# One block with the first shared pairs inside attention's last steps, and the second expert's result added by its transfer

## What is computed

```python
h = concat([patch_embed(x), text_embed(x_txt)])         # (64, 229, 128)
h = h + attn(layernorm(h))
t = layernorm(h)
# experts: 2 shared ones see every token, of 8 routed ones each token sees its 2 best
shared = sum_n gelu(t @ sw1[n].T + sb1[n]) @ sw2[n].T + sb2.sum(0)
probs  = softmax(t @ gate_w.T + gate_b);  top_v, top_i = top_k(probs, 2)
routed = sum_e cw[t, e] * (gelu(t @ rw1[e].T + rb1[e]) @ rw2[e].T + rb2[e])
out = h + shared + routed
```

## Time and profile before

| | |
|---|---|
| span of the profiled execution | 1363.1 us |
| that execution's own time | 1364.89 us |
| TensorE busy | 1231.9 us (90%) |
| VectorE | 1009.1 us (74%) |
| POOL | 830.3 us (61%) |
| ScalarE | 827.3 us (61%) |
| attention | 0 to about 581 us |
| early pairs | 590 to 799 us |
| routed tiles | 799 to 1204 us |
| late pairs | 1192 to 1363 us |

### The profile page before, as it was taken

The page is one execution under the profiler, slowest core; times in us unless marked ns, Lnnn a source line. Parts: engine busy times, 40 slices in busy tenths (PEclk is TensorE's granted clock), DMA queues, the critical chain, the costliest instruction groups (busy, mean ns, idle before and its releaser), DMA issues.

```text
span 1363.1 us, 39403 instructions
## 1 busy us (share of the span) xinstructions
PE 1231.9 (90%) x11910; PEld 1010.8 (74%) x11911; DVE 1009.1 (74%) x2599; ACT 827.3 (61%) x1969; POOL 830.3 (61%) x824
## 2 busy tenths in 40 slices
PE   4999999999999998257999989999999999998997
PEld 2777877777777886235777778888888888966676
DVE  3688788778788787238777757777777777789997
ACT  1566566565656665153444447777777777756664
POOL 3345776676767765667777616676676676753331
PEclk7999999999999999668999999999999999999999
DMA  5233334343333312124444222222222322236663
GB/s 153 81 126 112 116 117 128 100 132 114 120 113 125 127 60 69 61 81 132 121 115 119 73 57 81 83 84 81 82 84 76 86 81 80 64 99 179 187 179 106
DMA packets 119520, 142.62 MB, mean 105 GB/s; under 512 B 18591, under 2 KB 98782, under 8 KB 119417
## 3 DMA queue, kind: packets, MB, share of 16 engines
q1 hardware_dynamic: 95800, 101.42, 25.6%
q0 software_dynamic: 19584, 33.45, 8.1%
q10 hardware_dynamic: 4032, 6.57, 1.9%
HBM read 86.38 MB, written 55.96 MB: 104 GB/s over the span
## 4 chain that ended last, share of the span: by engine, by line
PE 45%; DVE 7%; issue 3%; ACT 2%; DMA 0%; POOL 0%; DVEq 0%; ACTq 0%
PE bank L1615 4%; PE bank L1637 4%; PE bank L1636 4%; PE bank L1638 4%; PE bank L1616 4%; PE bank L1617 4%; PE bank L1081 3%; PE bank L1080 3%; PE bank L1079 3%; PE bank L1033 2%; PE bank L1034 2%; DVE hid_all L1062 2%; PE bank L1035 2%; DVE hid_all L1064 2%; PE bank L1603 2%
## 5 line engine op out<-in xcount | busy, mean ns | idle before, releaser
L1334 POOL DMA_INDIRECT y_dram<-y_sb,y_row x244 | 273.1, 1119 | 154.5 <-issue 74.5
L1041 ACT ACTIVATE gel_all<-bank,b 128x458 f32<-128x458 f32 x256 | 157.1, 641 | 161.8 <-PE bank L1035 148.5
L1411 ACT ACTIVATE gel_all<-bank,b 128x256 f32<-128x256 f32 x488 | 192.9, 473 | 54.1 <-PE bank L1617 30.3
L1081 PE MATMUL bank<-w_hi,hid_all 128*117 128x128 f16 (+1 forms) x1024 | 181.5, 221 | 0.0
L1080 PE MATMUL bank<-w_lo,hid_all 128*117 128x128 f16 (+1 forms) x1024 | 181.4, 221 | 0.0
L1079 PE MATMUL bank<-w_hi,hid_all 128*117 128x128 f16 (+1 forms) x1024 | 181.4, 221 | 0.0
L1636 PE MATMUL bank<-w_hi,hid_all 128*128 x976 | 173.1, 220 | 0.0
L1637 PE MATMUL bank<-w_lo,hid_all 128*128 x976 | 170.5, 219 | 0.0
L1638 PE MATMUL bank<-w_hi,hid_all 128*128 x976 | 170.5, 219 | 0.0
L1534 DVE CAST hid_all<-gel_all 128x1024 f16<-128x1024 f32 x122 | 85.4, 700 | 103.3 <-ACT gel_all L1411 103.3
L1323 POOL DMA_INDIRECT slots_dram<-rows_s,slot_2nd x128 | 133.6, 1044 | 39.6 <-issue 38.3
(11 more groups left out here) (185 smaller groups left out, 3266.8 us busy)
## 6 DMA issues: line engine op xcount, KB each, us to landing
xin<-in_xmain SPq DMA_DIRECT2D x32, 771.8 KB
rows_r<-slots_dram SPq DMA_DIRECT2D x122, 130.0 KB
x2r_dram<-rows_1st SPq DMA_DIRECT2D x32, 260.0 KB, 2.6
rows_s<-x2r_dram SPq DMA_DIRECT2D x32, 260.0 KB, 2.7
scratch<-y_dram SPq DMA_DIRECT2D x32, 234.0 KB
x2t_dram<-x2T SPq DMA_DIRECT2D x32, 229.0 KB, 2.9
scratch<-y_dram SPq DMA_DIRECT2D x32, 224.0 KB
x_cols<-x2t_dram ACTq DMA_DIRECT2D x28, 229.0 KB, 2.7
```

The lines of the kernel that those rows point to most:

```text
L1081: last = pe.matmul(dst, lo, self.w_hi[:, w], start=False, stop=f == self.NG - 1)
L1334: pool.indirect_dma_start(out=y_dram, in_=y_sb[:, s, c, :], in_offset=None, out_offset=bass.IndirectOffsetOnAxis(ap=y_row[:, s, c:c + 1], ...
L1411: act.activation(gel[:, s8 % 2, f, :], up_bank[s8 % 2][half][:, (f % 2) * TILE:(f % 2 + 1) * TILE], ACT.Gelu, bias=b1[:, bass.ds((e + SHAR ...
```

## The change

- Both functions no longer open a block; they return each engine's function, and one block calls them one behind the other. The barrier between them goes. What the second part needs of the first, it now waits for by that part's semaphores.
- `steps` takes a function `between`, called behind steps 30 and later. SyncE loads the columns of pairs 0 and 1 behind step 30. Behind step 31 come pair 0's eight ups, gelus and four splits (now all on VectorE), behind step 32 the whole of pair 1 (`tensor_pair`, `vector_pair`), with pair 0's downs. VectorE's last `slots` and TensorE's last `rank` are in step 33, so behind pair 1.
- The two bias rows of the second layer (`b2`) are loaded and summed in attention's first steps, all on POOL (`sum_biases`, behind step -2); VectorE's part of it goes.
- In the second part VectorE's tables are cut into pieces between pairs 2, 3, 4, 5 and 6. POOL, not VectorE, clears `scratch`. `tag_rows` runs two rows later in the pairs, and SyncE writes the tails of the regions behind the load of pair 16, not 6.
- `rows_s` is now the same buffer as attention's `rows_1st`, so `load_rows` of the first four waits for attention's scatters. The PSUM banks are dealt out differently, so that pair 0's ups use banks that attention has left.
- `load_y` loads only the first result of each token; POOL issues a transfer that adds the second one (`accum_op`) in place of the sum.

```diff
-        embed_and_attend(nc, bank, ...)
-        experts_and_combine(nc, bank, ...)
+        attend, done = embed_and_attend(nc, keep, bank, ...)
+        experts = experts_and_combine(nc, keep, done, bank, ...)
...
+        @block.vector
+        def _(dve):
+            attend["vector"](dve, experts["vector_between"])
+            experts["vector"](dve)
...
             for i in range(hi, PAIRS + 4):
                 step(i, i % 2, i // 2, i % 4)
+                if between is not None and i >= PAIRS - 2:
+                    between(eng, i)
...
+            def sum_biases():
+
+                own = Own(pool, b2_up)
+                s0, s1 = EXPERTS * HID, (EXPERTS + 1) * HID
+                own.did(pool.memset(b2[:, :], 0.0))
+                pool.wait_ge(b2_loaded, 64)
+                own.did(pool.tensor_tensor(b2_in[:, s0:s1], b2_in[:, s0:s1], b2_in[:, s1:B2_COLS], ALU.add))
+                own.wait()
+                own.did(pool.tensor_copy(b2[0:B2_LO, :], b2_in[0:B2_LO, 0:s1]))
+                own.wait()
+                own.did(pool.tensor_copy(b2_high[B2_LO:, :], b2_in[B2_LO:, 0:s1]))
+                own.wait()
+                own.did(pool.tensor_tensor(b2[B2_LO:2 * B2_LO, :], b2_in[B2_LO:, 0:s1], b2_high[B2_LO:, :], ALU.subtract))
...
+    def up_free(self, pe, k, f):
+
+        if self.before is not None and isinstance(k, int) and k < 2 and f < (3 if k == 0 else 4):
+            if k == 0:
+                pe.wait_ge(self.before.sil, 5 * PAIRS)
+            else:
+                pe.wait_ge(self.gel_ready, self.NG)
+                pe.wait_ge(self.before.mid_ready, PAIRS)
+        elif self.before is not None and isinstance(k, int) and k == 0:
+            pe.wait_ge(self.gel_ready, f - 2)
...
+        def sync_between(sp, i):
+            if i == PAIRS - 2:
+                for k in range(2):
+                    sp.wait_ge(done.t_out[k], 16)
+                    early.load(sp, k, k)
...
+                else:
+                    sp.wait_ge(done.scattered[b], 64 * PAIRS // ROW_BUFS)
+                    sp.wait_ge(done.r_out[b], 16 * PAIRS // ROW_BUFS)
...
-                    sp.dma_start(y[0:n, b, :, c], y_v[i, at:at + n]).then_inc(y_in[b], 16)
+                    sp.dma_start(y[0:n, b, :, c, 0:HID], y_v[i, at:at + n, :, 0:HID]).then_inc(y_in[b], 16)
...
+            pool.memset(scratch[:, 1024:], 0.0).then_inc(scratch_up, 1)
...
-                both_y = y[:, b].rearrange("p i c w -> p (i c) w")
-                pool.tensor_tensor(both_y[:, :, 0:HID], both_y[:, :, 0:HID], both_y[:, :, HID:], ALU.add).then_inc(summed, 1)
+                for c, (at, n) in enumerate(CHUNKS):
+                    pool.dma_start(y[0:n, b, :, c, 0:HID], y_v[i, at:at + n, :, HID:], accum_op=ALU.add).then_inc(summed[b], 16)
...
+        def scalar_between(act, i):
+            if i == PAIRS - 1:
+                act.wait_ge(done.w_late, 16)
+                for f in range(NG):
+                    early.gelu(act, 0, f)
+                act.wait_ge(done.t_out[0], 32)
+                early.load(act, 2, 0)
...
+        def vector_between(dve, i):
+            if i == PAIRS - 1:
+                for j in range(NJ):
+                    early.split(dve, 0, 0, j)
+            if i == PAIRS:
+                vector_pair(dve, 1, 1)
...
+            dve.wait_ge(done.top_kept, PAIRS)
             dve.tensor_tensor(expd, top8[:, :, :], top8[:, :, 0:1].to_broadcast([P, NCH, 8]),
                               ALU.subtract).then_inc(centred, 1)
...
             dve.tensor_copy(tag_2nd[:, :, 1], expd[:, :, 1]).then_inc(tags_up, 1)
+            pair(2, 0)
...
+        def tensor_between(pe, i):
+            if i == PAIRS - 1:
+                pe.wait_ge(done.ws_done, PAIRS)
+                for f in range(NG):
+                    early.up(pe, 0, 0, f)
+            if i == PAIRS:
+                pe.wait_ge(done.b2_up, B2_STEPS)
+                tensor_pair(pe, 1, 1)
```

More of the change, by code:

```diff
@@ L15 @@
+from collections import namedtuple
 from contextlib import ExitStack
@@ L58 @@
 B2_LO = 32
+B2_COLS = (EXPERTS + SHARED) * HID
+B2_STEPS = 5
 EARLY_PAIRS = 18
@@ new lines, in build, with _ @@
+        block = keep.enter_context(nc.Block())
+        @block.sync
+        def _(sp):
+            attend["sync"](sp, experts["sync_between"])
+            experts["sync"](sp)
+        @block.gpsimd
+        def _(pool):
+            attend["gpsimd"](pool)
+            experts["gpsimd"](pool)
+        @block.vector
+        def _(dve):
+            attend["vector"](dve, experts["vector_between"])
+            experts["vector"](dve)
+        @block.scalar
+        def _(act):
+            attend["scalar"](act, experts["scalar_between"])
+            experts["scalar"](act)
@@ L271, in reaches, with steps @@
             return not isinstance(n, int) or n >= k
-        def steps(eng, step):
+        def steps(eng, step, between=None):
             lo, hi = 8, PAIRS - 8
@@ L327, in step, with gpsimd @@
                     store_x2(i - 1, 1 - p, (q - 1) % 4)
-            steps(sp, step)
-            for parity in range(2):
-                sp.wait_ge(t_out[parity], 16 * PAIRS // 2)
-            for buf in range(ROW_BUFS):
-                sp.wait_ge(r_out[buf], 16 * PAIRS // ROW_BUFS)
-                sp.wait_ge(scattered[buf], 64 * PAIRS // ROW_BUFS)
-            sp.wait_ge(w_late, 16)
-        @block.gpsimd
-        def _(pool):
+            steps(sp, step, between)
+        def gpsimd(pool):
             pool.memset(rel[:, :, :], 0.0).then_inc(zeroed, 1)
+            pool.memset(b2_in[:, 0:B2_COLS], 0.0).then_inc(b2_zeroed, 1)
             pool.memset(ident[:, :], 0.0).then_inc(const_p, 1)
@@ L461, in _, with vector @@
             steps(pool, step)
-        @block.vector
-        def _(dve):
+        def vector(dve, between):
             own = Own(dve, setup_v)
@@ L701, in _, with scalar @@
                                      op0=ALU.mult, op1=ALU.subtract).then_inc(uvw_ready, 1)
-            steps(dve, step)
-        @block.scalar
-        def _(act):
+            steps(dve, step, between)
+        def scalar(act, between):
             act.wait_ge(w_in, 16 * N_W)
@@ L819, in step, with tensor @@
                     weights_hi(i, p)
-            steps(act, step)
-        @block.tensor
-        def _(pe):
+            steps(act, step, between)
+        def tensor(pe, between):
             def text(grp):
@@ L998, in _ @@
             pe.wait_ge(setup_v, 9)
-            steps(pe, step)
+            steps(pe, step, between)
+    done = Done(t_out, r_out, scattered, ws_done, top_kept, slots_up, mid_ready, sil, x2T_ready, routed, lg_read, w_late, b2_up)
+    return {"sync": sync, "gpsimd": gpsimd, "vector": vector, "scalar": scalar, "tensor": tensor}, done
 class SharedExperts:
@@ L1005, with __init__ @@
     NJ = NG // 2
-    def __init__(self, nc, ctx, tag, first, flip, bank, acc, w_hi, w_lo, b1, b2, ones, x_cols, gel, hid, x2t_dram):
+    def __init__(self, nc, keep, tag, first, flip, up_bank, down_bank, acc, w_hi, w_lo, b1, b2, ones, x_cols, gel, hid, x2t_dram,
+                 before=None):
         def sem(name):
-            return ctx.enter_context(nc.semaphore(f"{name}_{tag}"))
+            return keep.enter_context(nc.semaphore(f"{name}_{tag}"))
         self.first, self.flip, self.acc, self.x2t_dram = first, flip, acc, x2t_dram
@@ L1296, in _ @@
             pool.memset(fill[:, :, HID:HID + 1], UNUSED).then_inc(filled, 1)
-            pool.memset(ones[:, :], 1.0).then_inc(set_up, 1)
             pool.iota(tile_no[:, :], pattern=[[1, TILES]], base=0, channel_multiplier=0,
@@ L1454, in _, with vector_pair, vector @@
             scale_y(PAIRS - 1)
-        @block.vector
-        def _(dve):
+        def vector_pair(dve, i, parity):
+            for j in range(NJ):
+                early.split(dve, i, parity, j)
+                if j == 2:
+                    early.accumulate(dve, i - 1, 0)
+            early.accumulate(dve, i - 1, 1)
+        def vector_between(dve, i):
+            if i == PAIRS - 1:
+                for j in range(NJ):
+                    early.split(dve, 0, 0, j)
+            if i == PAIRS:
+                vector_pair(dve, 1, 1)
+        def vector(dve):
             own = Own(dve, own_s)
```

272 lines of the change are left out of this document (120 added, 152 removed).

## The result

The changed kernel takes **1345.43 us** (median; 1344.18 to 1346.26), the kernel before 1364.57 in the same comparison: a ratio of 0.9862, 95% interval 0.9845 to 0.9879. The forecast was 1331, in a range of 1320 to 1352. So the time is in the range, but of the 34 us that the sum promised 19 came.

The account below looks back on a forecast made before the run. TensorE was taken as the bound, busy 90% of the span, with time to win only at the seam and in the last eighth. 22 us there plus 12 late made 34, so 1331 us from 1364.53, range 1320 to 1352.

Parts of the forecast that it names:

- rival (c): Seam: moved slots hold POOL and ScalarE longer, or the clock stays low; 12 us instead of 22, 1341 us; chance 0.13.
- seam wait of 24.2 us: Between the two blocks: TensorE waits for the second block's first columns, behind the barrier; the change was to remove it.
- one wait in pair 2: Seam: TensorE stands some 13 us at up(2, 4), for ScalarE's gelus behind the tags.
- first transpose: Start of the tiles: TensorE's first tile transpose was to come at 776 to 778.
- late period: Last stage: time per late pair was to be 10.6 to 10.8 us.
- they now begin ... 598.3 ... so its last one ends about 5 us before its 776.3, at 771.2: Seam: POOL's second-choice rows begin at 598.3 instead of 603.36, and end about 5 us earlier.
- up(3, 4): Early pairs after the seam: TensorE was to reach this up at 613.2 instead of about 639.4, gaining 26.2 us.
- if tags throttle TensorE ... 15: Seam, lower bound: tags throttling TensorE, or a clock slower to return, leave 15 us.
- 0, and 0 to 2 as bounds: Attention's start: bias loads and sums moved to the front cost 0, with 0 to 2 us as bounds.
- I take off 2: gain 12: Last stage: of at most 14.0 us, 2 go to the adding transfers' latency; gain 12, between 5 and 14.
- rival (a): Last stage: adding transfers become the bound, or five y buffers can't cover their latency; 1343 to 1363 us; chance 0.14.
- rival (b): Last stage: adding transfers cost from 2.55 us each, making the kernel slower; 1394 us at 3 us each; chance 0.06.

Follow-up runs that it names:

- rows_first: Changed kernel with SyncE's first four row loads ahead of the fill and POOL's scratch memset behind the first two pairs' scatters; 1346.35 us, ratio 0.9861.
- tails_last: Changed kernel with the eight fills of the regions' ends behind the last row load, run twice; ratios 0.9889 and 0.9882, second median 1350.78 us.
- ten_y: Changed kernel with ten half-width buffers for the experts' results in the same memory instead of five; 1340.22 us, ratio 0.983.
- y_plain: Changed kernel with POOL's 64 transfers overwriting instead of adding, so half of each expert sum is left out; 1339.95 us, ratio 0.9823.

## Why the prediction was right in sign and range, and its gain too large by 14 us

The time lies in the stated range, but outside what the forecast itself was given (1326 to 1339) and inside what rival (c) was given (1336 to 1346).

**Right: where the bound was, and that it moved.** The seam wait of 24.2 us and the table stall went, in their place came one wait in pair 2. The order at attention's end ran as followed, 3 to 5 us late throughout: the last slots at 586.8 (predicted 583.5), POOL's last first-choice row done at 597.6 (593.7), the first gelu of pair 2 begun at 604.8 (599.8: the prediction's 600.4 is its end), TensorE's wait 15.6 us (13). The four pieces of the tables cost TensorE at most 1.5 us of waiting (from 640 to 660), and the cast and the subtraction fell back to nearly their early times. Of the signs that were named, the first transpose (776 to 778, came at 791.3) and the late period (10.6 to 10.8 us, came at 11.0) were missed.

**Wrong: "they now begin ... 598.3 ... so its last one ends about 5 us before its 776.3, at 771.2".** This is the step that failed. It was right that POOL bounds the tiles' start; both terms of its chain were mis-sized. The start was 603.19, 4.9 late: 3.9 because the slots and the rows ahead of it were late, mostly attention's own 4.3, and 1.0 because the row load landed after about 4 us instead of the 2.7 of the earlier trace rows, and POOL waited for its tag. And the 128 transfers took 180.7 us from first to last, not 172.9: I took over the 1044 ns of the earlier trace rows, measured in the old order of work. In the new order the same transfer took 1109. The landing of the last row took 0.8 more than I allowed. That is 4.9 + 7.8 + 0.8 = 13.5 us, and tile 0 was issued at 787.36 instead of 773.9. What TensorE gained at up(3, 4) could not matter, for the reason that rows_first shows: TensorE is paced by POOL through the tags, and gives back what it gains. ScalarE began gelu(3, 4) at 619.2, 21.0 us earlier than before (26.2 was predicted, and 26.4 used in the next sum by a slip); at the tiles 8.3 were left. I had named this as a bound of the range ("if tags throttle TensorE ... 15"); the seam gave 12.6 by itself and 8.3 with the start, so the size is that of rival (c), 12 us; of its two reasons the late slots had a share, and the slower transfers were not among them.

What goes with the longer transfers can be read from the rows. In the changed kernel their mean is 1252 ns from 603 to 623 us and 1173 from 643 to 680, and falls to 1016 from 740 to 760, where before has 1017. One of the long ones, and VectorE beside it:

```profile
671.69 1.58 POOL L1352 DMA_INDIRECT slots_dram<-row_bufs,slot_2nd  x1 [0.30 <-issue]
```

```profile
671.30 1.11 DVE L1117 TENSOR_TENSOR hid_all<-gel_all,hid_all 128x916 f16<-128x916 f32 x1
```

The transfer begins 0.39 us into a subtraction and ends 0.86 us behind its end. That is the pattern of all that begin while VectorE is in a subtraction or a cast of the split: in the changed kernel they end 0.81 to 0.86 us behind its end (two 1.07), so the earlier in VectorE's instruction one begins, the longer it takes. The 44 that begin in a cast, which is short, take a mean of 1.13 us, the 19 in a subtraction 1.35 to 1.79, and the 65 in neither (or in its last 0.12 us) a mean of 0.97. Of the 128, only 6 begin in a subtraction in the kernel before, and 32 in tails_last_2. Thirteen more at some 0.56 us each are 7 of the 8.4 us. So the rows fit a POOL that stands until VectorE's instruction is over, and in the new order more transfers begin in a subtraction. Why they do, and whether moving them gives the time back, no run tells.

**Wrong for this profile: the start at "0, and 0 to 2 as bounds".** I asked who waits on POOL, and found nobody who needed it yet. The cost came from the side: VectorE's scalings, held off for 4.2 us, TensorE's wait of 3.2 us behind them, and some of it at the lower clock (granted 0.69 from 40 to 50 us, 1.00 before). What the start costs is 3.2 us in this profile; the other 1.1 of the 4.3 came at 522 to 528 us, where the granted clock was 0.50 for six microseconds, and I have no cause for that. In the profile of rows_first, with the same code, the start cost nothing, so the term varies from one execution to the next.

**Partly wrong: the late stage, "I take off 2: gain 12".** It gave 9.0. The issue was cheaper than I took (79.8 us for 64, 1.25 each, with 1.4 forecast), so rival (a) in its first form and rival (b) are out. The term that failed is the latency: I let the adding transfer land in 2.7 us, and it took 5.0 and 6.4. ten_y has the twelve pairs at 126.0 us, so what the latency cost is 5.8 us, not 2. That five buffers can't cover it stood in rival (a) as a side remark without a price. The Trainium skill's figure for a transfer issued by POOL beside a copy, 3.1 us ("SBUF — State Buffer", section "A bandwidth-pool intuition that's wrong (but worth ruling out)"), isn't borne out here: beside casts in every pair the issue took 1.25.

## What to carry to other kernels

When a chain that was hidden becomes the bound, its duration must not be taken from the time when it was hidden: 128 transfers at 1044 ns became 1109, with more of them begun inside a subtraction of VectorE, and that and the chain's later start were nearly the whole error at the seam. Before pricing a wait at its length, ask what the waiting engine is paced by; a wait of 6.4 us on ScalarE and 11 us of waiting on TensorE were each worth nothing here, because the same buffers held it up further on. And when a transfer takes over an engine's sum, size the buffers for its landing: the change gives half the buffer back, and using it for twice as many brought 5.9 us.

## What the runs showed of the hardware

- An adding transfer costs the DMA engines more than a plain one: 15867 packets and 47.2% of 16 engines for 6.86 MB, against 3401 and 21.3% for 7.13 MB, and lands after 5.0 to 6.4 us instead of 3.1 to 3.6. POOL takes 1.25 us to issue it instead of 0.74.
- DMA engines that are 98% busy (ten_y, 142.4 us) didn't slow the stage by a microsecond against 68% (y_plain, 141.8), as long as enough buffers were in flight.
- An indirect transfer that POOL begins while VectorE is in a cast or subtraction of the split ended, in the changed kernel, 0.81 to 0.86 us behind that instruction's end (two of 63 at 1.07); the 65 begun in neither took a mean of 0.97.
- VectorE's four scalings of 1.12 us took 5.30 beside POOL's casts and subtraction, and in the nine profiles with that overlap anything from 2.52 on.
- Chips differ: the same kernel before took 1365 us on one and 1502 to 1522 in three of the four sets, with waits put down to "remote" and "issue" on ScalarE (58.1 and 9.3 us in tails_last, 600 to 830 us). The cause is open.
